# Graph attention in another order: weights times input first, then the projection, in the steady turns of a four-layer graph network

## The reference

```
x = norm(x + gated neighbour sums)                       # L0
x = norm(x + two dense layers with batch statistics)     # L1
x = norm(x + attention(x))                               # L2
x = norm(x + h'), h' an LSTM over windows of 1 to 4 nodes
                  of two neighbour layers' output h      # L3
```

```
Wh = x @ W;  s1 = Wh @ a1;  s2 = Wh @ a2
e = leaky(s1[:, None] + s2[None, :]), -inf where adj == 0
x + softmax(e) @ Wh
```

## Time and profile before

| | us |
|---|---|
| median of 3 runs (lowest to highest) | 690.94 (690.61 to 691.45) |
| the profiled execution | 691.48 |
| its span in the profile | 689.6 |
| TensorE, VectorE, ScalarE, GpSimd busy | 647.0, 462.6, 405.2, 251.6 |

### The profile page before, as it was taken

The page is one execution under the profiler, slowest core; times in us unless marked ns, Lnnn a source line. Parts: engine busy times, 40 slices in busy tenths (PEclk is TensorE's granted clock), DMA queues, the critical chain, the costliest instruction groups (busy, mean ns, idle before and its releaser), DMA issues.

```text
span 689.6 us, 9202 instructions
## 1 busy us (share of the span) xinstructions
PE 647.0 (94%) x2818; PEld 444.7 (64%) x2818; DVE 462.6 (67%) x1338; ACT 405.2 (59%) x819; POOL 251.6 (36%) x250
## 2 busy tenths in 40 slices
PE   8899988996899999999999999999999999999993
PEld 6656646545675686578558757855875685576573
DVE  5968885678875567757765775677577665545444
ACT  3767765865745765575567546564754765546552
POOL 5787981005642023530443253144215413300301
PEclk9999999999999999999999999999999999999998
DMA  9223000000000000000000000000000000000000
GB/s 345 97 102 153 1 1 0 1 0 1 1 0 1 1 0 2 5 26 1 1 31 1 0 0 31 1 1 31 1 0 1 31 1 0 32 1 0 32 0 31
DMA packets 4225, 16.75 MB, mean 24 GB/s; under 512 B 464, under 2 KB 464, under 8 KB 4048
## 3 DMA queue, kind: packets, MB, share of 16 engines
q1 hardware_dynamic: 4176, 16.16, 6.1%
HBM read 11.97 MB, written 4.19 MB: 23 GB/s over the span
## 4 chain that ended last, share of the span: by engine, by line
PE 61%; DVE 9%; POOL 6%; ACT 4%; issue 3%; DVEq 0%; ACTq 0%; POOLq 0%
PE QQ L749 21%; PE QQ L761 13%; PE PA L732 4%; PE QQ L624 4%; POOL X L473 3%; PE PA L703 3%; POOL RSD L378 2%; PE PB L723 2%; PE PB L713 2%; DVE STL L1167 2%; PE PA L692 2%; PE PA L667 2%; PE PB L692 2%; PE PB L654 1%; ACT raw L1009 1%
## 5 line engine op out<-in xcount | busy, mean ns | idle before, releaser
L1009 ACT ACTIVATE raw<-QQ,BL 128x256 f32<-128x256 f32 (+2 forms) x312 | 167.1, 563 | 125.9 <-PE QQ L761 87.6
L749 PE MATMUL QQ<-HT,WT 128*128 128x256 f32 (+2 forms) x624 | 206.1, 473 | 5.7 <-DVE HT L1414 3.0
L378 POOL TENSOR_TENSOR RSD<-VAR,pw 128x8 f32<-128x8 f32 (+1 forms) x36 | 58.2, 1616 | 284.1 <-DVE VAR L1189 284.1
L749 PEld LDWEIGHTS QQ<-HT,WT 128*128 128x128 f32 x624 | 115.8, 190 | 69.3 <-issue 31.6
L761 PE MATMUL QQ<-HB,WT 128*128 128x256 f32 (+2 forms) x384 | 114.1, 440 | 1.9 <-DVE HB L1414 1.9
L1396 DVE SCALAR_TENSOR_TENSOR raw<-raw 128x512 f32<-128x512 f32 (+2 forms) x88 | 50.5, 574 | 69.0 <-ACT raw L1009 68.4
L761 PEld LDWEIGHTS QQ<-HB,WT 128*128 128x128 f32 x384 | 70.4, 190 | 34.5 <-issue 15.3
L1016 ACT ACTIVATE raw<-raw 128x512 f32<-128x512 f32 (+2 forms) x88 | 45.1, 513 | 44.8 <-DVE raw L1406 32.5
L492 POOL TENSOR_TENSOR HB<-HB 128x512 f32<-128x512 f32 x28 | 35.2, 1275 | 91.4 <-ACT HB L968 91.4
L1414 DVE SCALAR_TENSOR_TENSOR HB<-raw 128x256 f32<-128x256 f32 (+2 forms) x48 | 24.0, 499 | 29.3 <-ACT raw L1016 29.3
L1414 DVE SCALAR_TENSOR_TENSOR HT<-raw 128x512 f32<-128x512 f32 (+2 forms) x40 | 25.0, 625 | 27.8 <-ACT raw L1016 27.8
(11 more groups left out here) (180 smaller groups left out, 1068.4 us busy)
## 6 DMA issues: line engine op xcount, KB each, us to landing
raw<-in_xt SPq DMA_DIRECT2D x8, 512.0 KB, 6.5
four<-in_x SPq DMA_DIRECT2D x8, 512.0 KB, 5.1
out<-four SPq DMA_DIRECT2D x7, 512.0 KB, 2.6
WT<-in_lstm SPq DMA_DIRECT2D x1, 2048.0 KB, 7.8
later<-in_later SPq DMA_DIRECT2D x1, 662.0 KB, 9.1
AD<-in_adj SPq DMA_DIRECT2D x1, 512.0 KB, 5.6
out<-four SPq DMA_DIRECT2D x2, 256.0 KB, 2.1
early<-in_early SPq DMA_DIRECT2D x1, 274.0 KB, 3.0
```

Source lines behind the costliest of these rows:

```text
L378: pool.tensor_tensor(RSD[kk][:, ts], VAR[kk][:, ts], pw[:, ts], ALU.pow).then_inc(ln[k]["rstd"], some)
L749: mm = pe.matmul(steps_view(Q[q], k), WT[:, 0, (p - 1) * 4 + q, :], ht_view(par, k), start=True, stop=(s == 0))
L1009: act.activation(TG[q][:, 0:n], Q[q][:, 0:n], ACT.Tanh, scale=0.5 if q == G else 0.25, bias=BL[:, p - 1, q:q + 1]).then_inc(g_ok, 1)
```

## The change

In the turns (groups 2 to 7) the weights are multiplied with the normalised input X2 first (`a_mix`), ScalarE copies the product (`a_mixed`), and the projection W follows (`a_project_mix`). The softmax's sums come from the exponentials' accumulator output (DEN), with one reciprocal for a group. s1 and s2 are sixteen dot products on VectorE (`a_dots`) of the rows before the norm with the centred vectors W a1 and W a2, then scaled by 1/sqrt of the variance (`a_s12`); TensorE turns the s2 column, repeated 128 times, into rows (`a_rows`). The centred vectors are made once, beside the output product of L1. ScalarE, and not VectorE, normalises X2 (`norm_apply`), for which GpSimd also makes the offset (L384). The transposing of X2, its copy, the scores and the first projection go. Groups 0 and 1 keep the old way.

Orders that change: on VectorE `a_sum1` stands between cell 0 and its state, `t_sum` and `t_norm` later, `a_biased0` after step 4, and the second norm is done in two halves around step 10. On GpSimd `weights` stands before `tail`, and `scale2` of the own group at the turn's end in two halves. On TensorE `h(3)` stands before `weigh0`; the spread is split 2 + 2. On ScalarE `a_relu` stands after the gates of step 5. The core of the diff:

```diff
-                if k == 0 or (k == 1 and g < 2) or (k == 3 and g == GROUPS - 1):
+                if k in (0, 1) or (k == 3 and g == GROUPS - 1):
...
             def slot(s, par, A, B, L, T):
-                if B:
-                    scale2(s - 1)
                 if A:
                     rstd(1, 0, s)
+                    weights(s, range(GB))
                 if T:
                     tail(s - 3, 1 - par)
                 if A:
-                    weights(s, range(GB))
                     scaled(s + 2)
-                    rstd(2, 1, s)
+                    for h in range(2):
+                        rstd(2, 1, s, h)
+                        scale2(s, h)
...
+            scale2(1)
...
-            spin(Q[3][:, 0:P], 14)
+            for k in range(2):
+                mm = pe.matmul(Q[3][:, k * P:(k + 1) * P], AR[:, k * P:(k + 1) * P], WTR, start=True, stop=True)
+            spin(Q[3][:, 2 * P:3 * P], 12)
...
+                    pe.wait_ge(rows_ok, 1) if (g, q) == (1, 1) else None
...
+            def a_rows(g):
+                pe.wait_ge(s12_ok, g - 1)
+                reach(pe, sp_ok, 2 * g)
+                for b in range(GB):
+                    for c in range(NC):
+                        t = 2 * b + c
+                        mm = pe.transpose(turned(PA, c, b), S12[:, 1, t:t + 1].broadcast_to([P, P]), ident[:])
+                mm.then_inc(s2_ps, 2)
...
+                        pe.wait_ge(wh_ok, NC * (g + 1)) if g < 2 else pe.wait_ge(max_ok, TILES * (g + 1))
...
+            def a_mix(g, some):
+                pe.wait_ge(ln[1]["out"], TILES * (g + 1))
+                f = front(g)
+                for b in some:
+                    pe.wait_ge(pt_ok, GB * g + b + 1)
+                    for m in range(NC):
+                        mm = pe.matmul(f.AB[b][:, 0:NODES], turned(X2, m, b), f.MS[:, 2 * b + m, :],
+                                       start=(m == 0), stop=(m == NC - 1))
+                    mm.then_inc(px_ps, 1)
+            def a_project_mix(g, some):
+                f = front(g)
+                for b in some:
+                    pe.wait_ge(px_ok, GB * (g - 2) + b + 1)
+                    for c in range(NC):
+                        at = NODES + c * P
+                        mm = pe.matmul(f.AB[b][:, at:at + P], turned(f.X2T, c, b), WX[:, 0:P], start=True, stop=True)
+                    mm.then_inc(att_ps, 1)
...
-                pe.wait_ge(max_ok, upto(g + 2) * TILES) if g else None
...
-                pe.wait_ge(wh_ok, upto(g + 2) * NC) if g else None
+                pe.wait_ge(max_ok, upto(g + 2) * TILES) if g else None
...
                 a_residual(s) if A else None
                 x(1)
                 t_turn(s - 3, 1 - par) if T else None
-                a_spread0(s - 1, (0, 1, 2)) if B else None
+                a_spread0(s - 1, (0, 1)) if B else None
                 x(2)
-                a_spread0(s - 1, (3,)) if B else None
+                a_spread0(s - 1, (2, 3)) if B else None
                 x(3)
-                a_turn(s) if A else None
+                h(3)
+                a_rows(s) if A else None
                 a_weigh0(s - 1) if B else None
-                h(3)
-                if A:
-                    a_project(s, 0)
-                    a_scores(s)
-                    a_project(s, 1)
                 x(4)
                 x(5)
                 h(5)
...
                 a_turn_e(s, range(GB)) if A else None
                 h(8)
                 x(9)
-                a_attend(s, (0, 1, 2)) if A else None
+                if A:
+                    a_mix(s, (0, 1, 2))
+                    a_project_mix(s, (0, 1))
                 h(9)
                 x(10)
-                a_attend(s, (3,)) if A else None
+                if A:
+                    a_mix(s, (3,))
+                    a_project_mix(s, (2,))
                 h(10)
+                a_project_mix(s, (3,)) if A else None
...
+            def a_mixed(g, some):
+                f = front(g)
+                for b in some:
+                    act.wait_ge(px_ps, GB * (g - 2) + b + 1)
+                    act.activation(f.X2T[:, b * NODES:(b + 1) * NODES], f.AB[b][:, 0:NODES], ACT.Copy).then_inc(px_ok, 1)
...
-                        e = act.activation(f.E1[:, t], f.E1[:, t], ACT.Exp, bias=f.EB[:, t:t + 1], scale=SLOPE)
+                        e = act.activation(f.E1[:, t], f.E1[:, t], ACT.Exp, bias=f.EB[:, t:t + 1], scale=SLOPE,
+                                           accum_out=DEN[:, t:t + 1] if g > 1 else None)
...
@@ -1030,14 +1065,12 @@
                 cell(1)
                 cell(2)
                 a_spread(s - 1) if B else None
-                a_turned(s) if A else None
-                gates(3)
-                a_projected(s, 0) if A else None
-                state(3)
-                a_projected(s, 1) if A else None
+                norm_apply(1, 0, Z, s, X2) if A else None
+                cell(3)
+                cell(4)
+                gates(5)
                 a_relu(s - 1) if B else None
-                cell(4)
-                cell(5)
+                state(5)
                 a_lin(s, (0, 1, 2)) if A else None
                 cell(6)
                 if A:
@@ -1046,7 +1079,9 @@
                 cell(7)
                 a_exps(s, (2, 3)) if A else None
                 cell(8)
+                a_mixed(s, (0, 1, 2)) if A else None
                 cell(9)
+                a_mixed(s, (3,)) if A else None
                 cell(10)
...
+            dve.wait_ge(out2_ps, 1)
+            done(dve.tensor_reduce(WAM[:], Q[3][:, 0:2 * P].rearrange("p (k f) -> p k f", k=2), AX.X, ALU.add))
+            done(dve.tensor_scalar(WAM[:], WAM[:], -1.0 / P, None, ALU.mult))
+            done(dve.tensor_scalar(WAR[:, 0, :], Q[3][:, 0:P], WAM[:, 0:1], None, ALU.add))
+            dve.tensor_scalar(WAR[:, 1, :], Q[3][:, P:2 * P], WAM[:, 1:2], None, ALU.add).then_inc(rows_ok, 1)
...
+            def a_dots(g):
+                dve.wait_ge(z1_ok, 2 * (g + 1))
+                dve.wait_ge(rows_ok, 1)
+                for k, junk in enumerate((one_a, one_c)):
+                    for t in range(TILES):
+                        dve.tensor_tensor_reduce(nth(junk, t), nth(Z, t), WAR[:, k], 1.0, 0.0,
+                                                 ALU.mult, ALU.add, DOT[:, k, t:t + 1]).then_inc(dots_ok, 1)
+            def a_s12(g):
+                dve.wait_ge(dots_ok, 2 * TILES * (g - 1))
+                dve.wait_ge(ln[1]["rstd"], 2 * (g + 1))
+                dve.tensor_tensor(S12[:], DOT[:], RSD[0][:].unsqueeze(1).broadcast_to([P, 2, TILES]), ALU.mult).then_inc(s12_ok, 1)
...
+                rows = f.PB if g < 2 else PA
...
+                dve.wait_ge(wh_ok, halves(g, h)) if g < 2 else dve.wait_ge(s12_ok, g - 1)
...
+                s1 = f.WH[:, ts, P] if g < 2 else S12[:, 0, ts]
...
+            def a_inverse(g):
+                dve.wait_ge(exps_ok, GB * (g + 1))
+                dve.reciprocal(RD[0][:], DEN[:]).then_inc(rd_ok, GB)
+            def a_sum2_mix(g, some):
+                f = front(g)
+                for b in some:
+                    dve.wait_ge(att_ps, GB * g + b + 1)
+                    dve.wait_ge(rd_ok, GB * (g + 1))
+                    for c in range(NC):
+                        at = NODES + c * P
+                        dve.scalar_tensor_tensor(out=turned(f.Z2, c, b), in0=f.AB[b][:, at:at + P],
+                                                 scalar=RD[0][:, 2 * b + c:2 * b + c + 1], in1=turned(X2, c, b),
+                                                 op0=ALU.mult, op1=ALU.add).then_inc(z2_ok, 1)
...
+                inner(0)
                 a_sum1(s) if A else None
+                state(0)
                 cell(1)
-                t_sum(s - 3) if T else None
                 a_norm1(s) if A else None
                 cell(2)
-                a_apply1(s) if A else None
-                t_norm(s - 3) if T else None
-                a_biased0(s - 1) if B else None
+                t_sum(s - 3) if T else None
+                if A:
+                    a_dots(s)
+                    a_s12(s)
                 cell(3)
                 a_max(s) if A else None
                 cell(4)
+                a_biased0(s - 1) if B else None
                 a_bias(s) if A else None
                 cell(5)
+                t_norm(s - 3) if T else None
                 a_biased1(s - 1) if B else None
                 cell(6)
                 a_hidden(s - 1, 1 - par) if B else None
@@ -1450,13 +1523,14 @@
                 cell(8)
                 if A:
                     a_weights(s, (2, 3))
-                    a_sum2(s, (0, 1, 2))
+                    a_inverse(s)
+                    a_sum2_mix(s, (0, 1))
                 cell(9)
                 if A:
-                    a_sum2(s, (3,))
-                    a_stats2(s)
+                    a_norm2(s, 0)
+                    a_sum2_mix(s, (2, 3))
                 cell(10)
-                a_small2(s) if A else None
```

(51 more changed lines are left out.)

51 lines of the change are left out of this document (18 added, 33 removed).

## The result

The changed kernel takes 688.83 us as a median of 8 runs (688.36 to 689.51), the one before 690.78 beside it (690.30 to 691.63): a ratio of 0.9974, 95% interval 0.9964 to 0.9984. That is 1.9 us less, where 8.6 were forecast.

The account below looks back on a forecast made before the run. TensorE, busy 94% of the span, was taken as the bound. Five full turns save 6.5 us, the first 0.8, the seventh 1.5: 8.8, less 0.2 for centred vectors, 8.6; forecast 682.5 us, range 675 to 691.

Parts of the forecast that it names:

- The gaps eat the saving: Rival: longer waits for the exponentials' sums and at step 2 leave 0.15 a turn, 688 us in all; chance 0.17.
- TensorE's work, 1.86 less a turn: TensorE in a full turn: 8.03 us of work goes out, 6.17 comes in, 1.86 saved.
- Dots, 0.22 from start to start, covered by 1.6: VectorE's sixteen dot products take 3.5 us; the scaled column is ready at T+19.3, TensorE asks for it at 20.9.
- the first rival, the dots: Rival: dots at a pitch above 0.28 delay step 3's state; 695 us at 0.42, 703 at 0.50; chance 0.08.
- Step 2's wait, 1.0: TensorE before step 2, with only two spread batches ahead: ready at T+8.7, waits until 9.7, a new gap of 1.0.
- The rival of GpSimd's tiles blocking step 10's cell: Rival: four cell operations each stand behind a 0.56 tile, adding 2.2; 4 us slower, 695; chance 0.05.
- Step 4's gap, 0.4: TensorE before step 4: ready at T+23.6, step 3's state comes at T+23.9, a gap of 0.4 with the release.
- The tail's norm (2.7) now stands before biased1, and the second spread comes 0.4 late: VectorE after step 5: the norm takes 2.7 us ahead of biased1, delaying TensorE's second spread by 0.4.
- From step 8 on all is covered: End of the turn: mixed copies fall into ScalarE's free stretches; the last projection ends 0.45 behind step 10's matmuls.
- the sums of the exponentials: ScalarE's accumulator read, taken as 0.08 per exponential; the third and fourth transposes of exponentials wait 0.35 in all.
- The seventh turn, 1.5: Turn without stage A: shorter gaps save 1.9, less 0.4 for the later norm, giving 1.5 us.
- the 1.88 against 0.29 near the start: Two L1134 instructions: one took 1.88, its twin 0.29, read as a two-SBUF-input instruction standing still behind GpSimd's 2.04 multiplication.

Follow-up runs that it names:

- run 6: The late-norm kernel (tail norm's parts moved into VectorE's idle time) with the sixteen dot products done twice: 693.01 us, ratio 1.0031.
- Runs 1 and 9: Changed kernel, GpSimd's weights held: in the first until the tail norm's variance is there, 688.77 us; in the second until step 6's cell is formed, 685.81 us.
- Run 4: Changed kernel with the tail norm split, its statistics and small operations moved into VectorE's idle time, so biased1 follows step 5 at once: 680.53 us.
- Run 7: Kernel before, without the new algebra, with the tail's norm moved ahead of biased1 and GpSimd's weights ahead of its tail: 700.38 us.
- run 2: Changed kernel with each of GpSimd's additions L498 of groups 2 to 7 cut into two of 256 columns: 688.88 us, ratio 0.9983.
- run 5: The late-norm kernel with three batches of the spread before step 2 and one after step 3's place, instead of 2 + 2: 674.60 us.
- run 8: The late-norm, three-batch-spread kernel with step 7's gates on ScalarE put before the second batch of exponentials: 675.55 us, ratio 0.9782.

## Why the prediction was wrong

The direction was right, the size wrong by 6.7 us, nearly all of it in one term. The time fell where the rival *The gaps eat the saving* had put it (688), but by a wait that this rival didn't name, so its number was luck. By the prediction's own steps:
- *TensorE's work, 1.86 less a turn*: right, 60.58 to 58.78, 1.80. The repeated column costs what ordinary data costs (L682, eight in 0.87).
- *Dots, 0.22 from start to start, covered by 1.6*: right, 0.21 to 0.22, sixteen from 402.58 to 406.06; the scaled column is there at T+19.2, the transposes start at 20.9. So the first rival, the dots, fell, and run 6 shows where it would have begun.
- *Step 2's wait, 1.0*: 0.86 in the turn shown (394.05 + 1.73 to 396.64), released by the state of step 1 as forecast. The rival of GpSimd's tiles blocking step 10's cell fell: its three operations took 0.46, 0.59 and 0.48 there instead of 0.42 each, 0.3 in all and not 2.2.
- *Step 4's gap, 0.4*: right, 0.48 (408.78 + 1.72 to 410.98).
- *"The tail's norm (2.7) now stands before biased1, and the second spread comes 0.4 late"*: the step that failed. The norm took 4.5, from 420.27 to 424.73, and the spread came 1.97 late. Runs 1 and 9 have the norm in that same place with GpSimd quiet: 2.5, and no wait at all. What is missing, 1.6 a turn against the forecast, is GpSimd's addition standing in the way of two small operations, a meeting that the forecast put at nothing. Over five full turns it is 7.9, against the 7.0 by which they missed their forecast (0.5 longer than before, where 6.5 less was said). Run 4 took the norm and the meeting away and came to 680.5, inside the forecast's own range of 678 to 687. Run 7 put the meeting into the kernel before.
- *"From step 8 on all is covered"* and the sums of the exponentials: each takes 0.49 from start to start instead of 0.40, near the 0.08 taken. The transposes were to wait 0.35 in all; the fourth does, 0.37 (433.82 + 0.44 to 434.63). Once the norm was moved (run 4), part of it showed elsewhere, in the 0.5 wait for step 7's gates.
```profile
434.63 0.66 PE L698 MATMUL PA<-ident,HB 128*128 128x128 f32 x4 [0.20 <-ACT HB L1012]
```
- *The seventh turn, 1.5*: 1.64.

The cause was in sight. The prediction read the 1.88 against 0.29 near the start as an instruction standing still behind GpSimd's, and the trace of before has a first cell operation that took 0.83 instead of 0.51, beside an addition (L492) that ran until 428.75; this is its row, which the prediction didn't show:
```profile
428.28 0.83 DVE L1396 SCALAR_TENSOR_TENSOR raw<-raw 128x340 f32<-128x340 f32 x1 [0.44 <-ACT raw L1009]
```
I checked the dots and step 10's cell against GpSimd's work, and not the norm, which had met nothing: in the kernel before, GpSimd waited idle for its VAR. When both orders changed, the additions came to run beside it.
```profile
408.27 1.64 POOL L378 TENSOR_TENSOR RSD<-VAR,pw 128x8 f32<-128x8 f32 x1 [5.31 <-DVE VAR L1189]
```
The rule of the Trainium skill ("SBUF — State Buffer", section "Who interferes with whom"), an exclusive lock for the whole instruction, gives the measured stalls of the two-input operations: by it an operation that arrives while a 1.25 addition runs waits for its end, and run 2's halved instructions gave halved stalls. Where I let the 0.1 of step 3's cells stand for the usual price, I had taken short tiles as the measure for long additions.

Left open: why short tiles cost so little. Beside the tail's tiles (0.66 on average in the kernel before) VectorE's cells lose 0.1, beside instructions of 1.2 up to 1.1, whether these have two tensor inputs (L498) or one (L471, run 9). A wait to the end of a tile would cost more than 0.1 on average. Nor is it the length of the record alone: run 2's pieces are 0.69 long, hardly more than a tile, and stalled small operations by 0.5. The tiles themselves lengthen: the tail's eight took 5.27 beside step 3's cells in the kernel before, and 3.79 in the changed kernel's turn, where they stand elsewhere (431.79).
```profile
410.01 5.27 POOL L484 TENSOR_SCALAR four<-HB,MEAN,RSD 128x128 f32<-128x128 f32 x8
```
So part of the price of such a meeting is paid by GpSimd. One reading of the rest is an estimate that no run tests: L471 takes 1.19 for 1024 columns and the shortest tile 0.44 for 128, about 0.11 for each further 128 columns, so that most of a tile's record would be a fixed part; if only the remainder kept VectorE out, the loss would be about 0.1. No run changed the tiles.

## What to carry to other kernels

When an order is changed on VectorE or GpSimd, lay their two timelines side by side and check every pair that newly meets; the small operations of a norm are bad to have beside long GpSimd instructions, since each may wait for the end of one. Taking 3% off the bound engine's work gained nothing in the full turns until the step that stood in the way was put into idle time; after that run 5's move was worth in a turn what its row said, and run 8's was worth nothing. Holding the other engine back moved the meeting to other work (runs 1 and 9: 0 and 3 us gained, of some 8); moving the sensitive work to where it isn't awaited removes its cost.

## What the runs showed of the hardware

- VectorE operations on 8 or 16 columns, 0.16 to 0.17 alone, took 1.12 to 1.21 beside GpSimd additions of 1.25, and 0.64 to 0.70 beside pieces of 0.69; one with a single input was among these. One on 4 columns took 1.05 beside a one-input GpSimd instruction of 1.19 (run 4).
- The accumulator read of ScalarE, 48 of them in the changed kernel:
```profile
L1012 ACT ACTIVATION_READ_ACCUMULATOR HB<-HB,EB 128x1 f32 x48 | 9.0, 187 | 0.0
```
  Its record is 0.19, and by the spacing of the exponentials it lengthens an exponential by 0.09 from start to start.
- The dot product over 128 columns has a record of 0.29 and repeats each 0.21, its accumulator read of 0.08 included.
